# The attention tokens turned to channels by DMA instead of TensorE, and their low part made on GpSimd

## What is computed

```python
x = x + conv_experts(group_norm(x))              # 4 experts, 96 -> 96 -> 96, gated per position
t = to_tokens(x)                                 # (32, 784, 96)
n1 = layer_norm(t)
qkv = n1 @ qkv_w + qkv_b                         # 12 heads of 8
A = feature(k)^T @ feature(v) * gauss            # 8x8 per head, over all 784 tokens
t = t + (q @ (A - lambda * A)) @ proj_w + proj_b
n2 = layer_norm(t)
t = t + quantized_mlp(n2)                        # 96 -> 384 -> gelu -> 96, each followed by a scale by a
                                                 # group's largest absolute value (groups of 6 images)
```

## Time and profile before

| | us |
|---|---|
| median of 3 runs | 779.37 (778.01 to 780.0) |
| the profiled execution's own time | 777.66 |
| its span, first to last instruction | 776.0 |
| TensorE busy | 727.5 (94%) |
| VectorE busy | 679.7 (88%) |
| ScalarE busy | 473.3 (61%) |
| GpSimd busy | 221.5 (29%) |
| mean granted TensorE clock | 0.977 |

### The profile page before, as it was taken

One profiled execution on the slowest core, in us unless ns is written; L12 is line 12 of the kernel. 1 busy time (PEld: TensorE's weight loads), 2 busy tenths in 40 slices (PEclk: granted clock), 3 DMA queues, 4 the chain that ended last, 5 costly groups with the idle time before them and its releaser, 6 DMA issues.

```text
span 776.0 us, 15540 instructions
## 1 busy us (share of the span) xinstructions
PE 727.5 (94%) x4858; PEld 480.5 (62%) x4858; DVE 679.7 (88%) x2058; ACT 473.3 (61%) x669; POOL 221.5 (29%) x301
## 2 busy tenths in 40 slices
PE   6798899999999999999999999999999899999991
PEld 3465466666766666766666766666766566555550
DVE  3577589999999999999999999999999678999997
ACT  2455356665555665555665555665554699999980
POOL 2352223324333324333324333324332001111110
PEclk8889899999999999999999999999999999999996
DMA  9970111111111111111111111111110101564446
GB/s 216 199 186 1 32 33 32 34 47 31 31 47 31 31 47 31 31 47 31 31 47 31 31 47 31 31 47 31 31 31 16 31 1 19 91 127 60 62 63 140
DMA packets 17663, 41.40 MB, mean 53 GB/s; under 512 B 4553, under 2 KB 4839, under 8 KB 17639
## 3 DMA queue, kind: packets, MB, share of 16 engines
q1 hardware_dynamic: 14552, 33.27, 16.4%
q0 software_dynamic: 2688, 7.23, 6.6%
q10 hardware_dynamic: 399, 0.60, 0.3%
HBM read 22.28 MB, written 18.67 MB: 53 GB/s over the span
## 4 chain that ended last, share of the span: by engine, by line
PE 63%; DVE 18%; issue 6%; ACT 5%; SPq 3%; DMA 2%; POOL 2%; DVEq 1%; ACTq 0%; POOLq 0%
PE slot L1071 15%; PE slot L1055 13%; PE slot L1284 6%; PE slot L1077 5%; PE slot L917 5%; PE slot L1082 5%; PE slot L1131 5%; DVE stage L1659 4%; PE slot L1118 4%; ACT stage L799 4%; SPq L476 3%; DVE stage L1646 3%; DVE y2max L1765 2%; DVE xn L1788 1%; PE slot L1342 1%
## 5 line engine op out<-in xcount | busy, mean ns | idle before, releaser
L1071 PE MATMUL slot<-hT,w2s 128*96 128x392 f32 x372 | 132.6, 492 | 0.8 <-DVE w2s L1532 0.8
L1613 DVE TENSOR_SCALAR tok<-tok,ln_mv,ln_rs 112x96 f32<-112x96 f32 x434 | 109.0, 322 | 2.0 <-POOL ln_rs L624 1.9
L624 POOL TENSOR_TENSOR ln_rs<-ln_ve,pow_half 112x7 f32<-112x7 f32 (+2 forms) x92 | 105.1, 1142 | 7.2
L799 ACT ACTIVATE stage<-slot,kv_bias,kv_unit 112x768 f32<-112x768 f32 (+1 forms) x62 | 53.1, 907 | 86.6 <-PE slot L1118 86.6
L621 POOL TENSOR_TENSOR ln_ve<-ln_mv,ln_eps 112x7 f32<-112x7 f32 (+2 forms) x92 | 18.3, 199 | 296.1 <-DVE ln_mv L1595 296.1
L792 ACT ACTIVATE hT<-slot,b1c,w_unit 128x784 f32<-128x784 f32 x93 | 93.1, 1004 | 15.8 <-PE slot L1055 13.2
L1082 PE MATMUL slot<-big,W1b 96*128 (+1 forms) x360 | 89.3, 329 | 0.0
L1071 PEld LDWEIGHTS slot<-hT,w2s 128*96 128x96 f32 x372 | 58.6, 163 | 45.0 <-issue 42.9
L1619 DVE TENSOR_REDUCE ymax<-slot 128x784 f32 (+1 forms) x90 | 84.5, 966 | 0.0
L1077 PE MATMUL slot<-big,W1b 99*128 (+1 forms) x360 | 84.4, 329 | 0.0
L854 ACT ACTIVATE hT<-slot,s 128x784 f32<-128x784 f32 x90 | 80.2, 914 | 6.1 <-DVE stage L1646 3.2
(11 more groups left out here) (252 smaller groups left out, 1455.4 us busy)
## 6 DMA issues: line engine op xcount, KB each, us to landing
xs<-in_x SPq DMA_DIRECT2D x32, 294.0 KB, 2.9
out<-h_second SPq DMA_DIRECT2D x32, 294.0 KB, 2.6
big<-in_x SPq DMA_DIRECT2D x7, 1176.0 KB, 15.5
out<-h_second POOLq DMA_DIRECT2D x24, 294.0 KB, 4.2
big<-out SPq DMA_DIRECT2D x1, 1764.0 KB, 10.5
out<-big SPq DMA_DIRECT2D x6, 294.0 KB, 2.7
big<-in_x SPq DMA_DIRECT2D x2, 588.0 KB, 24.5
con<-shape_consts ACTq DMA_DIRECT2D x1, 445.5 KB, 6.3
```

What stands on the lines that cost most here:

```text
L624: nc.gpsimd.tensor_tensor(ln_rs[n][:, j0:j1], ln_ve[n][:, j0:j1], pow_half[0:TOK, j0:j1], ALU.pow).then_inc(ln_rstd[part], 1)
L799: nc.scalar.activation(ekv[:, j0:j0 + n, :], chunks(k, n, 256, 2 * C), ACT.Exp, bias=kv_bias[:, :], scale=kv_unit[0:TOK, 0:1]).then_inc(e_ ...
L1071: ins = mm(S[k][0:C, h, 0:HALF], w2s[:, v, t, :], src[:, t, h * HALF:(h + 1) * HALF], start=t == 0, stop=t == last, skip_group_check=True)
L1613: ins = V.tensor_scalar(src[:, j, :], src[:, j, :], ln_mv[n][:, j, 0:1], ln_rs[n][:, j:j + 1], ALU.subtract, ALU.mult)
```

## The change

Tokens are turned to channels by two transposing DMAs, and no longer by TensorE. ScalarE casts tok1 (still as tokens, in SBUF) to x1_hi; GpSimd subtracts to x1_lo; SyncE moves each with one `dma_start_transpose` to xh1_hi and xh1_lo. A chunk in x1_hi has 128 columns: 96 channels, a column of ones (which gives xh1_hi its row for the bias) and zeros; these pads are set once in the setup. TensorE waits for the transfers' semaphores, x1_hi_moved and x1_lo_moved. VectorE's subtraction goes, and so do the seven transposes in slot 0. The high part's transfer also waits for ao_ready of the image before, since attention_out still reads the buffer. To make room, some setup buffers share memory (by_channel, by_row). SyncE's loop is written out image by image. In `stats2` the aggregation of the first four chunks moves ahead of the fifth chunk's statistics. Where TensorE had transposes at the start and the end of the fused stage, it has more filling matmuls (`keep_busy`).

```diff
+            def move_x1(i):
+                sp.wait_ge(x1_hi_ready, i)
+                if isinstance(i, int) and i == 1:
+                    sp.wait_ge(pads_ready, 1)
+                else:
+                    sp.wait_ge(ao_ready, i - 1)
+                sp.dma_start_transpose(turned(xh1_hi[:, 0:HW]),
+                                       x1_hi[:, :, :].rearrange("p j c -> p (j c)")).then_inc(x1_hi_moved, 16)
+                sp.wait_ge(x1_lo_ready, i)
+                sp.dma_start_transpose(turned(xh1_lo[:, 0:HW]),
+                                       x1_lo[:, :, :].rearrange("p j c -> p (j c)")).then_inc(x1_lo_moved, 16)
...
+                    move_x1(2 * m + r)
                     load_next(m, r)
                     store_last(m, r)
...
+            then(nc.gpsimd.memset(x1_lo[:, :, C:P], 0.0))
+            then(nc.gpsimd.memset(x1_hi[:, :, C:P], 0.0))
+            nc.gpsimd.memset(x1_hi[:, :, C:C + 1], 1.0).then_inc(pads_ready, 1)
...
+            def x1_low(i):
+                pool.wait_ge(x1_hi_ready, i)
+                nc.gpsimd.tensor_tensor(x1_lo[:, :, 0:C], tok1[:, :, :], x1_hi[:, :, 0:C],
+                                        ALU.subtract).then_inc(x1_lo_ready, 1)
+
             def step(m, r, next_=True):
                 i = 2 * m + r
+                if not isinstance(i, int) or i >= 1:
+                    x1_low(i)
                 if not isinstance(i, int) or i >= 2:
                     rstd(1, i - 2)
                     rstd(2, i - 2)
...
-            def xh1_high(i):
-                act.wait_ge(x1T_ready, i)
-                nc.scalar.copy(*channels(xh1_hi[0:C, 0:HW], 0)).then_inc(xh1_hi_ready, 1)
+            def x1_high(i):
+                act.wait_ge(xh1_ready, i)
+                nc.scalar.copy(x1_hi[:, :, 0:C], tok1[:, :, :]).then_inc(x1_hi_ready, 1)
...
+                if attend:
+                    x1_high(i)
                 if experts and not between and not early:
                     relu(2, 2)
                 if attend:
-                    xh1_high(i)
                     exp_kv(0, 3, 0, CH_A)
...
-                pe.wait_ge(xh1_lo_ready, done)
+                pe.wait_ge(x1_lo_moved, 16 * done)
...
-                if attend and not second:
-                    x1_to_channels()
...
-                    pe.wait_ge(xh1_hi_ready, i)
+                    pe.wait_ge(x1_hi_moved, 16 * i)
...
                 chunk_stats(tok2, range(CH_A)).then_inc(ln_stats[1], 1)
+                moments(1, f + 1)
                 chunk_stats(tok2, range(CH_A, CH_A + 1))
-                moments(1, f + 1)
...
-                if attend:
-                    dve.wait_ge(xh1_hi_ready, i)
-                    V.tensor_tensor(tokenwise(xh1_lo[:, 0:HW]),
-                                    flat(0)[0:C, 0:CHUNKS * P].rearrange("p (j t) -> p j t", t=P)[:, :, 0:TOK],
-                                    tokenwise(xh1_hi[0:C, 0:HW]), ALU.subtract).then_inc(xh1_lo_ready, 1)
```

More of the change, by code:

```diff
@@ L159, in build, with token_part @@
         ident = con[:, K_ID:K_ID + P]
-        w1_raw = sb("w1_raw", [P, TILES, C])
-        w2_raw = sb("w2_raw", [C, E, C])
+        by_channel = sb("by_channel", [P, 3 * HID])
+        w2_raw = by_channel[0:C, 0:HID].rearrange("p (e d) -> p e d", e=E)
+        W2_raw = by_channel[0:C, HID:2 * HID]
+        part_b = by_channel[:, 2 * HID:3 * HID]
+        by_row = sb("by_row", [P, 2, TILES, C])
+        w1_raw = by_row[:, 0, :, :]
+        W1_raw = by_row[:, 1, :, :]
+        TOKENS = CHUNKS * P // 2
+        def token_part(view):
+            return view.bitcast(F16).rearrange("p (j c) -> p j c", c=P)
+        x1_lo = token_part(by_channel[0:TOK, 0:TOKENS])
+        x1_hi = sb("x1_hi", [TOK, CHUNKS, P], F16)
         w1_max = sb("w1_max", [P, TILES])
@@ L191, in build @@
         wmean = sb("wmean", [P, 2, QGROUPS])
-        part_b = sb("part_b", [P, HID])
         part_h = sb("part_h", [P, HID], BF16)
@@ L257, in build @@
         tok2 = sb("tok2", [TOK, CHUNKS, C])
-        xh1_hi = sb("xh1_hi", [C + 1, HW + P - TOK], F16)
-        xh1_lo = sb("xh1_lo", [C, HW + P - TOK], F16)
+        xh1_hi = sb("xh1_hi", [P, HW + P - TOK], F16)
+        xh1_lo = sb("xh1_lo", [P, HW + P - TOK], F16)
         w_max = sb("w_max", [C + 1, W_KINDS])
@@ L384, in build @@
         xh2_ready = sem("xh2_ready")
-        x1T_ready = sem("x1T_ready")
-        xh1_hi_ready = sem("xh1_hi_ready")
-        xh1_lo_ready = sem("xh1_lo_ready")
+        x1_hi_ready = sem("x1_hi_ready")
+        x1_lo_ready = sem("x1_lo_ready")
+        x1_hi_moved = sem("x1_hi_moved")
+        x1_lo_moved = sem("x1_lo_moved")
+        pads_ready = sem("pads_ready")
         w_max_ready = sem("w_max_ready")
@@ L509, in _ @@
                         store_last(m, r)
-            with sp.Fori(FIRST // 2, LAST // 2 - 1) as m:
+            for m in range(FIRST // 2, LAST // 2 - 1):
                 for r in range(2):
+                    move_x1(2 * m + r)
                     load_next(m, r)
@@ L514, in _ @@
             for r in range(2):
+                move_x1(LAST - 2 + r)
                 store_last(LAST // 2 - 1, r)
+            move_x1(LAST)
             store_last(LAST // 2, 0)
@@ L543, in _ @@
             nc.gpsimd.memset(xh1_hi[0:C, HW:], 0.0).then_inc(ones_ready, 1)
-            nc.gpsimd.memset(xh1_lo[:, HW:], 0.0).then_inc(ones_ready, 1)
+            nc.gpsimd.memset(xh1_lo[0:C, HW:], 0.0).then_inc(ones_ready, 1)
             nc.gpsimd.memset(zg[:, :, :, :].rearrange("p a j w -> p (a j w)"), 0.0).then_inc(ones_ready, 1)
@@ L616, in _ @@
             nc.gpsimd.tensor_scalar(kv_bias[:, :], kv_bias[:, :], -1.0, 1.0, ALU.add, ALU.mult).then_inc(kvw_ready, 1)
+            pool.wait_ge(kvw_ready, 2)
+            pool.wait_ge(setup_T, 1)
+            pool.wait_ge(bigones_ready, 16)
+            then(nc.gpsimd.memset(x1_lo[:, :, C:P], 0.0))
+            then(nc.gpsimd.memset(x1_hi[:, :, C:P], 0.0))
+            nc.gpsimd.memset(x1_hi[:, :, C:C + 1], 1.0).then_inc(pads_ready, 1)
+            pool.wait_ge(pads_ready, 1)
             def rstd(part, b):
@@ L645, in _ @@
             step(LAST // 2 - 1, 1, next_=False)
+            x1_low(LAST)
             for r in range(2):
@@ L1145, in last_attend @@
                 keep_busy(1, 0, 8)
-                pe.wait_ge(xh1_ready, BATCH)
-                to_channels(0, tok1, x1T_ready)
                 y1_max_row()
-                keep_busy(1, 0, 2)
-                pe.wait_ge(xh1_hi_ready, BATCH)
+                keep_busy(1, 0, 12)
+                pe.wait_ge(x1_hi_moved, 16 * BATCH)
                 pe.wait_ge(t2_ready, BATCH - 1)
@@ L1210, in step @@
                     hidden(2, 2, r)
-                def x1_to_channels():
-                    pe.wait_ge(xh1_ready, i)
-                    to_channels(0, tok1, x1T_ready)
                 if second:
```

17 lines of the change are left out of this document (8 added, 9 removed).

## The result

The changed kernel takes **803.29 us** (median of 4 runs, 801.18 to 805.48) against 778.69 us of the kernel before (4 runs, 776.81 to 780.0) on the same chip. The ratio is **1.0318, with a 95% interval from 1.0276 to 1.036**. Forecast were 812 us and a range of 777 to 860. The direction, the mechanism and the range held.

What follows compares the result with a forecast made beforehand. TensorE and VectorE were both full, the period F-a plus about 10.4 us. F-a = 4.12+3.1 = 7.22, 0.99 more in 30 images: 777.66+29.7+0.9+2.6 = 810.9, with 1.7 for the runs' median 812 us; range 777 to 860.

Steps and rivals of the forecast that it cites:

- The period is F-a plus 10.4: Fused stage, per image: the part after the feature map's start stays about 10.4 us, so only F-a changes the period.
- F-a: VectorE, from tok1's normalization end (a) to the feature map's start (F): 6.23 us before, 7.22 forecast.
- TensorE's 0.67 us: Seven transposes fewer on TensorE save 0.67 us per image, but this saving is not collected.
- ScalarE's cast, GpSimd's subtraction: Per image, the cast from SBUF takes 0.75 us and the new subtraction of 672 columns 1.47 us.
- GpSimd's path: Subtraction, then roots, then tok2's last chunks and t1cm on VectorE: F-a of 6.46 us, 0.23 more than before.
- SyncE's queue: Queue free; high part's transfer issued 0.97 us and low part's 2.51 us after tok1's normalization, with 0.16 us SyncE delay.
- T: SyncE's transposing transfer, from issue to landing: 3.1 us taken, between a low end of 1.7 and a high of 4.2.
- 1309 ns for each 128x128: Slow transfers, seven chunks one after another: transfer 9.2 us, whole near 1000 us; chance 0.02.
- the two terms of 0.9 and 2.6 us: Extra time at the ends: 0.9 us for the first attention image, 2.6 us for the last.
- Fast transfers: Rival: transposing transfers as fast as plain ones (T under 2.34), GpSimd's path sets F-a to 6.46: 788 us; chance 0.22.
- Faster: Rival: TensorE's saving comes through, F-a under 6.23, T under 2.1: 759 us fully collected, 775 partly; chance 0.12.

Runs made afterwards that it cites:

- experiment 2: Changed kernel with GpSimd subtracting only one chunk of tok1 out of seven, every wait and transfer kept: 795.55 us.
- experiment 5: Changed kernel with both transfers as plain copies of 784 columns in place of turning the tokens: 788.80 us.
- experiment 7: Changed kernel with cast and GpSimd's subtraction in two pieces, the first cast piece starting once chunks 0 to 3 of tok1 are normalized: 784.29 us.
- experiment 4: Changed kernel with cast, subtraction and both transfers cut into chunks 0 to 3 and 4 to 6, VectorE subtracting the second half: 847.96 us.
- experiment 1: Changed kernel with GpSimd's subtraction moved behind the two pairs of roots: 933.83 us, ratio 1.2008.
- experiment 10: Changed kernel with TensorE's seven transposes of tok1 put back in 30 images, their result read by nobody: 801.28 us.
- experiment 6: Changed kernel with the cast in two pieces, GpSimd subtracting chunks 0 to 3 and VectorE 4 to 6, transfers whole: 799.82 us.
- experiment 9: Kernel before the change, with only VectorE's first moments of the second LayerNorm moved ahead of chunk 4's statistics: 777.69 us, ratio 1.0001.
- Experiment 3: Changed kernel with the last image's two transfers ahead of the store on SyncE's queue and nine more dummy products in image 2: 801.68 us.
- experiment 12: Changed kernel with early cast cut behind chunk 5, nine dummy products in image 2, last image turned by TensorE as before the change: 782.21 us.

## Why the prediction was right, and where it was off

**The period is F-a plus 10.4.** Right in the changed kernel, 6.73+10.40 = 17.13 (measured 17.12), and with 6.50 in experiment 2 (16.92), 6.39 in experiment 5 (16.77) and 6.20 in experiment 7 (16.60). Two experiments show its limits. In experiment 4 F-a fell to 5.90, but the second k,v group waited for its own transfers and the period rose to 18.3 on average: the second part is 10.4 only while the second group's inputs are there with the first's. In experiment 1, where TensorE had waited 3.41 us and ran at 0.58, the second part took 12.76.

**TensorE's 0.67 us aren't collected.** Right, and shown by experiment 10.

**ScalarE's cast, GpSimd's subtraction.** 0.75 and 1.47 us forecast; 0.75 and 1.46 measured.

**GpSimd's path.** F-a = 6.46 forecast. In the trace t1cm, which ends this path, ends at 324.65+1.02 = 325.67, a+6.47; the feature map then waited 0.25 us more for the exponential. Without that wait it overlaps t1cm's end, and the path gives 6.39 (experiment 5). VectorE's wait for the roots was 1.50, forecast 1.7.

**SyncE's queue.** The low issue came at a+2.35, forecast a+2.51: the 0.16 us for SyncE's delay, taken from a load that waits for VectorE, was 0.02 here. And the issue's own 1.21 us, four times what a load takes, was not in the working. It didn't show in the changed kernel, because the subtraction ran beside it. It was what set the low issue in experiments 2, 4, 6 and 7.

**T.** Forecast 3.1, measured 2.76. These two terms account for the size of the steady loss: 0.16+0.34 = 0.50, so F-a grew by 0.50 in place of 0.99. Experiment 5 prices the turning at 0.4 us over a plain transfer of seven eighths of the columns. The Trainium skill (Advanced Engine Details and Errata, X-Bar Transpose) has turning transfers as fast as regular ones; in landing that is nearly so here (2.8 against 2.4), on the issuing queue it is not (1.21 against 0.52). The other figure of it that the prediction named, 1309 ns for each 128x128 (VectorE: DVE Perf Modes, The three transpose paths), doesn't add up over chunks: seven land after 2.8 us, four after 2.4.

**The ends.** This is the step that failed, and with it the two terms of 0.9 and 2.6 us. The sum gave the first attention image 0.9 us and the last 2.6, and every image between them the steady rate. Measured are 9.3 us by the seventh t1cm, where the steady excess would be some 3, and 6.3 at the end. The first term was also read from behind a slow stretch: in the trace of before the clock is 0.67 from 85 to 90 us, TensorE came late to the transposes, and the third product stood 4.72 us behind tok1. In experiment 9, at 1.00, it is 2.84 us; the changed kernel has 5.15. Three more things were missing. "The store of the image before follows h_second, which VectorE makes ahead of tok1's normalization, so the queue is free" is false for the last image, where h_second comes behind tok1 (626.71 against 623.87, and in the trace of before, where it could have been read, 605.17 against 602.34): 1.8 us of delay for the high transfer. The subtraction's effect on VectorE's other operations was not asked about. And the clock was left out: behind a wait of 1.9 us in image 2 and of 2.3 us in the last, TensorE's rows show 0.50 to 0.73. Experiment 3 took up the first and the last of these (the third product 2.2 us sooner, more filling for TensorE) and brought 1.6 us in all, which lies within the spread of the runs.

So for the profiled execution, at 805.5 us against a sum of 810.9, the steady loss was taken 12 us too large (25 images at 0.50) and the ends 7 us too small. That the sum came within 5.4 us is owed to these two going against each other.

**The rivals.** Fast transfers (788) needed T under 2.34; experiment 5, at 2.4 and 788.8 us, is that case all but reached. "Faster" needed T under 2.1 and a shorter GpSimd path, and no version came there.

**What stays open.** Why the clock falls in one of two like stretches (experiments 9 and 12), and so how much of the ends' cost belongs to the change. Why single transfers land late: the median of both kinds is 2.8 us and the least 2.7, but in the kernel after one low part took 3.9 (issued 147.08) and one high part 4.3 (issued 165.21), followed by waits of 1.85 and 1.66 us on TensorE, the first of them by a clock of 0.51 and 0.64 in the next 4 us, the second by none lower than 1.00; in other versions it is other images, and in experiment 5 one plain transfer took 3.1. Two queues for the two parts were not tried: the Trainium skill (DMA: Bandwidth & Descriptors, Silent corruption: two transposing streams in flight at once) says that such streams can damage both outputs unless one waits for the other, and no run here shows it.

## What to carry to other kernels

Before a step is moved to an engine with room, draw its new path from the last producer to the first reader and count every link, the queue's hold and the landing too; that sum decides, not the busy shares. A fixed price per transfer speaks against cutting it up and for starting its inputs earlier: begun on the first chunks, the same transfers cost 19 us less in all. And look at the first and the last round by themselves: there the order of the queue and the clock are others than in the steady one.

## What was not expected of the hardware

- A transposing transfer from SBUF to SBUF held SyncE's queue 1.19 to 1.26 us whether it moved three, four or seven chunks; a plain one of 784 columns held it 0.52.
- GpSimd's subtraction, with two inputs in SBUF, stretched VectorE's operations that ran beside it: seven normalizations from 1.93 to 3.02 us (experiment 1), and a 112x112 operation with two inputs to 1.29 us, where the ones behind it took 0.26. In that second case VectorE's operation ended 0.14 us behind GpSimd's. The Trainium skill (SBUF — State Buffer, SBUF: two separate sides) describes an exclusive lock on a port pair that the two engines share, held against VectorE's operations in a two-port mode or with two inputs in SBUF, so that the one that comes second waits for the other's end; both rows agree with it. The statistics of three chunks were not stretched: 0.55 us beside the subtraction and, in experiment 1, without it.
- TensorE's granted clock fell to 0.57 or 0.58 behind the wait of 3.41 us in experiment 1, and the rest of the round took 11.3 to 12.8 us in the steady images for 10.40. The whole lost 130 us to a step moved by some 3 us in 30 images, half again what the moving alone comes to (30 times 2.7 to 3.0).
